# One ring of three PSUM banks for all background products, and both heads of a maximum unit as two 64-row products

## The reference

```
keys = einsum("bse,neh->bsnh", residual, W_key) + Bias_key          # queries, values alike
scores = einsum("bknh,bqnh->bnqk", keys, queries) / sqrt(H)
scores = where(q_idx < k_idx, 1e-10, scores)
probs = softmax(scores, axis=3)
weighted = einsum("bnqk,bknh->bqnh", probs, values)
out = einsum("bqnh,nhe->bqe", weighted, W_output) + Bias_output
x = x + attention(layernorm(x)); x = x + ffn(layernorm(x))          # ffn: 3 blocks of dequantised + low-rank linears
```

## Time and profile before

| | us |
|---|---|
| median of 3 runs | 2510.45 (2510.26 to 2524.81) |
| profiled execution, its own time | 2510.64 |
| its span | 2508.9 |
| attention, first score product to last weighted sum | 190.3 to 2117.6 |

### The profile page before, as it was taken

The page is one execution under the profiler, slowest core; times in us unless marked ns, Lnnn a source line. Parts: engine busy times, 40 slices in busy tenths (PEclk is TensorE's granted clock), DMA queues, the critical chain, the costliest instruction groups (busy, mean ns, idle before and its releaser), DMA issues. The chain is left out here.

```text
span 2508.9 us, 30066 instructions
## 1 busy us (share of the span) xinstructions
PE 2276.1 (91%) x9988; PEld 1172.2 (47%) x10080; DVE 1502.6 (60%) x3928; ACT 815.9 (33%) x1166; POOL 1183.0 (47%) x1075
## 2 busy tenths in 40 slices
PE   3479999999999999999999999999999997699987
PEld 2214444444444444444444444444444443577765
DVE  3584757575656565656565656666666665166664
ACT  1103333343333343433333333343333343001111
POOL 0105565656565657474747474747474720111110
PEclk8669999999999999999999999999999999799998
DMA  4463353626263536353544444444545341612100
GB/s 135 145 143 94 89 147 82 152 75 154 73 154 86 141 93 168 99 128 102 124 107 120 113 114 121 107 125 106 128 99 135 89 120 39 218 44 100 59 18 17
DMA packets 205354, 273.58 MB, mean 109 GB/s; under 512 B 69200, under 2 KB 86800, under 8 KB 205200
## 3 DMA queue, kind: packets, MB, share of 16 engines
q1 hardware_dynamic: 205200, 271.67, 41.4%
HBM read 176.69 MB, written 94.63 MB: 108 GB/s over the span
## 5 line engine op out<-in xcount | busy, mean ns | idle before, releaser
L691 POOL TENSOR_TENSOR acc<-acc,probs 128x512 f32<-128x512 f32 (+1 forms) x900 | 998.7, 1144 | 411.9 <-ACT probs L918 411.9
L918 ACT ACTIVATE probs<-ps_s 128x1024 f32<-128x1024 f32 (+2 forms) x640 | 552.6, 897 | 384.7 <-PE ps_s L780 230.2
L778 PE MATMUL ps_s<-qq,kk 128*128 128x512 f32 (+3 forms) x1280 | 638.3, 499 | 30.7 <-ACT probs L918 30.7
L967 DVE TENSOR_REDUCE partial<-ps_bg 128x1 f32<-128x512 f32 x768 | 513.6, 687 | 197.8 <-PE ps_bg L723 128.7
L799 PE MATMUL ps_o<-probs,v 128*64 128x512 f32 (+3 forms) x2560 | 537.8, 541 | 2.4 <-issue 2.4
L780 PE MATMUL ps_s<-qm,kl 128*128 128x512 f32 (+3 forms) x1280 | 468.4, 366 | 0.0
L723 PE MATMUL ps_bg<-k_bf,q_pad 128*128 128x512 bf16 (+3 forms) x1188 | 404.3, 362 | 57.3 <-DVE partial L967 18.8
L710 PE MATMUL ps_bg<-xs,w_in 128*128 128x512 f32 x768 | 366.9, 602 | 21.2 <-DMA xs<-xn_turned 18.8
L778 PEld LDWEIGHTS ps_s<-qq,kk 128*128 128x128 f32 x1280 | 247.4, 193 | 192.2 <-issue 118.5
L964 DVE CUSTOM_DVE_ANT_0 junk<-ps_bg,mask_q 128x512 bf16<-128x512 f32 (+3 forms) x512 | 242.4, 486 | 100.2 <-issue 94.1
L684 POOL TENSOR_TENSOR acc<-probs 128x512 f32<-128x512 f32 x90 | 112.8, 1275 | 401.1 <-ACT probs L918 401.1
(11 more groups left out here) (103 smaller groups left out, 1681.1 us busy)
## 6 DMA issues: line engine op xcount, KB each, us to landing
high_and_low<-split SPq DMA_DIRECT2D x128, 512.0 KB, 5.4
qq<-high_and_low SPq DMA_DIRECT2D x64, 512.0 KB, 4.7
kk<-high_and_low SPq DMA_DIRECT2D x128, 256.0 KB, 5.6
qm<-high_and_low SPq DMA_DIRECT2D x64, 256.0 KB, 6.3
kl<-high_and_low SPq DMA_DIRECT2D x64, 256.0 KB, 6.8
e<-masked_weights SPq DMA_DIRECT2D x128, 128.0 KB, 2.9
scale<-inverse_sums SPq DMA_DIRECT2D x128, 128.0 KB, 2.9
heads_turned<-o_out SPq DMA_DIRECT2D x64, 256.0 KB, 2.2
```

The lines of the kernel that those rows point to most:

```text
L691: g.tensor_tensor(acc[h][:, group % 2, q0:q0 + w], acc[h][:, group % 2, q0:q0 + w], probs[h][:, probs_slot(i, t), at:at + w], ALU.add).the ...
L778: pe.matmul(out, kk[:, h, kb * P:(kb + 1) * P], qq[:, h, q], start=True, stop=False, skip_group_check=True)
L918: nc.scalar.activation(probs[h][:, probs_slot(i, t), 0:width], ps_s[:, h, 0:width], ACT.Exp, scale=SCORE_SCALE).then_inc(p_ready, 1)
L967: e.reduce_max(to, ps_bg[:, n % 2, 0:w], AX.X).then_inc(max_read, 1)
```

## The change

It does three things.
- `ps_bg` gets three banks and `ps_fin` goes: projections, units, transposes and denominators take the three banks in turn, in the order in which TensorE issues them. A function `background` writes that order down, and every use waits for the reader of the use three before it.
- `q_pad` becomes one `q_bf` of both heads, as `k_bf` is. A unit is now both heads: two products over 64 rows each (`HEAD`), rows 0 to 63 and 64 to 127, into two banks in succession. There are 40 units for 80.
- The units start at slot 11 and end at slot 115. They take the keys of the last chunk first, so that each needs only the projections done by then.

```diff
-MAX_UNITS = [(h, qb, u, min(CH, 128 * (qb + 1) - CH * u))
-             for c in GROUPS for qb in range(4 * c + 3, 4 * c - 1, -1) for u in range(c + 1) for h in range(2)]
+MAX_UNITS = [(qb, u, min(CH, 128 * (qb + 1) - CH * u))
+             for c in GROUPS for u in range(c, -1, -1) for qb in range(4 * c + 3, 4 * c - 1, -1)]
...
-MAX_AT = [n + (n % 6 == 4) for n in range(MAX_SLOT, MAX_SLOT + NMAX)]
+MAX_AT = [11, 13, 15, 17, 19, 21, 25, 27, 29, 31, 33, 35, 38, 41, 44, 47, 50, 53, 56, 59, 61, 65, 68, 71, 75, 77, 80, 85,
+          87, 89, 92, 95, 97, 99, 101, 104, 109, 111, 113, 115]
...
+def background(n_pairs_in_all):
+    order = [("proj", 0, u) for u in range(NPROJ)] + [("max", 0, n) for n in range(NMAX)]
+    order += [(kind, 0, c) for kind, c in FIN_FIRST]
+    for i in range(n_pairs_in_all):
+        for n in range(SLOTS + 1):
+            if i + 1 < n_pairs_in_all:
+                order += [("proj", i + 1, u) for u in range(NPROJ) if PROJ_SLOT[u] == n]
+                order += [("max", i + 1, v) for v in range(NMAX) if MAX_AT[v] == n]
+            order += [(kind, pair_of(i, kind, c), c) for kind, c, at in FIN
+                      if at == n and pair_of(i, kind, c) < n_pairs_in_all]
+    first, users, counts = {}, [], {"proj": 0, "max": 0, "fin": 0}
+    for use in order:
+        kind = use[0] if use[0] in counts else "fin"
+        first[use] = len(users)
+        for _ in range(2 if kind == "max" else 1):
+            counts[kind] += 1
+            users.append((kind, counts[kind]))
+    return first, users
...
-        ps_bg = ctx.enter_context(nc.psum_tensor("ps_bg", [P, 2, CH], F32))
+        ps_bg = ctx.enter_context(nc.psum_tensor("ps_bg", [P, BANKS, CH], F32))
-        ps_fin = ctx.enter_context(nc.psum_tensor("ps_fin", [P, CH], F32))
+        place, users = background(N)
...
+                def bank_read(kind, j, n, h=0):
+                    k = place[kind, j, n] + h
+                    if k >= BANKS:
+                        reader, count = users[k - BANKS]
+                        pe.wait_ge({"proj": proj_read, "max": max_read, "fin": fin_read}[reader], START + count)
...
                 def max_unit(j, n):
-                    h, qb, u, w = MAX_UNITS[n]
...
-                    pe.matmul(ps_bg[:, n % 2, 0:w], q_pad[h][:, qb * P:(qb + 1) * P], k_bf[:, CH * u:CH * u + w],
-                              start=True, stop=True).then_inc(max_scores, 1)
+                    qb, u, w = MAX_UNITS[n]
+                    pe.wait_ge(bf_ready, START + 4 * j + PROJ_CHUNKS.index(u) + 1)
+                    for h in range(2):
+                        bank_read("max", j, n, h)
+                        pe.matmul(bank("max", j, n, h)[:, 0:w], q_bf[HEAD[h], qb * P:(qb + 1) * P],
+                                  k_bf[HEAD[h], CH * u:CH * u + w], start=True, stop=True).then_inc(max_scores, 1)
...
-                        for h in range(2):
-                            own = slice(64 * h, 64 * h + 64)
-                            e.tensor_copy(q_pad[h][own, cols(c)], part[own, 0, :].bitcast(F32))
+                        e.tensor_copy(q_bf[:, cols(c)], part[:, 0, :].bitcast(F32))
...
-                for h in range(2):
-                    e.memset(q_pad[h][:, :], 0.0)
```

More of the change, by code:

```diff
@@ L350, in attention @@
         vt = sb("vt", [P, S])
-        q_pad = [sb(f"q_pad{h}", [P, S], BF16) for h in range(2)]
+        q_bf = sb("q_bf", [P, S], BF16)
         k_bf = sb("k_bf", [P, S], BF16)
@@ L438, in fin_index, with bank @@
             return [e[:2] for e in FIN].index((kind, c))
+        def bank(kind, j, n, h=0):
+            return ps_bg[:, (place[kind, j, n] + h) % BANKS, :]
         def nth(i, group):
@@ L815, in between @@
                             continue
-                        before = fin_before(i, k)
                         if kind == "vt":
-                            turn_values(c, before)
+                            turn_values(values_pair(i, kind, c), c)
                         elif kind == "den":
-                            denominators(i, c, before)
+                            denominators(i, c)
                         else:
-                            turn_max(i + 1, c, before)
+                            turn_max(i + 1, c)
                 for u in range(NPROJ):
@@ L828, in _ @@
                     max_unit(0, n)
-                for k, (kind, c) in enumerate(FIN_FIRST):
+                for kind, c in FIN_FIRST:
                     if kind == "mt":
-                        turn_max(0, c, k)
+                        turn_max(0, c)
                     else:
-                        turn_values(c, k)
+                        turn_values(0, c)
                 for h in range(2):
@@ L944, in low @@
                     part = split[u // 3 % 2]
-                    e.scalar_tensor_tensor(part[:, 2 * m + 1, :], ps_bg[:, u % 2, :], bias[:, m:m + 1],
+                    e.scalar_tensor_tensor(part[:, 2 * m + 1, :], bank("proj", j, u), bias[:, m:m + 1],
                                            part[:, 2 * m, :].bitcast(F32), ALU.add, ALU.subtract
@@ L957, in take_max @@
                 def take_max(j, n):
-                    h, qb, u, w = MAX_UNITS[n]
-                    dve.wait_ge(max_scores, START + NMAX * j + n + 1)
-                    if u == qb // 4:
-                        e.memset(wait_here[:, n % 4:n % 4 + 1], 0.0)
-                    to = partial[:, h, qb, u:u + 1]
-                    if u == qb // 4:
-                        e.tensor_tensor_reduce(junk[:, n % 2, 0:w], ps_bg[:, n % 2, 0:w], mask_q[:, CH - w:CH], 1.0,
-                                               3 * NEVER, ALU.add, ALU.max, to).then_inc(max_read, 1)
-                    else:
-                        e.reduce_max(to, ps_bg[:, n % 2, 0:w], AX.X).then_inc(max_read, 1)
-                    c = qb // 4
+                    qb, u, w = MAX_UNITS[n]
+                    c = qb // 4
+                    for h in range(2):
+                        of = bank("max", j, n, h)[:, 0:w]
+                        k = (place["max", j, n] + h) % BANKS
+                        to = partial[:, h, qb, u:u + 1]
+                        dve.wait_ge(max_scores, START + 2 * (NMAX * j + n) + h + 1)
+                        if u == c:
+                            e.memset(wait_here[:, k:k + 1], 0.0)
+                            e.tensor_tensor_reduce(junk[:, k, 0:w], of, mask_q[:, CH - w:CH], 1.0,
+                                                   3 * NEVER, ALU.add, ALU.max, to).then_inc(max_read, 1)
+                        else:
+                            e.reduce_max(to, of, AX.X).then_inc(max_read, 1)
                     if n == LAST_MAX[c]:
-                        dve.wait_ge(max_read, START + NMAX * j + n + 1)
+                        dve.wait_ge(max_read, START + 2 * (NMAX * j + n + 1))
                         e.tensor_reduce(neg_max[:, c, :].rearrange("p (h r) -> p h r", h=2),
```

50 lines of the change are left out of this document (22 added, 28 removed).

## The result

| | median us | lowest to highest | n |
|---|---|---|---|
| before | 2512.02 | 2510.26 to 2524.81 | 6 |
| changed | 2444.61 | 2440.23 to 2557.76 | 6 |

The changed kernel is faster: ratio 0.9712, 95% interval 0.9681 to 0.9743. Predicted were 2448 us in a range of 2420 to 2530. In a second series the ratio is 0.9713 (0.9684 to 0.9742). All readings of "the changed kernel" here are from a profiled execution of the second series, span 2441.3 us.

What follows compares the result with a forecast made beforehand. TensorE's queue was taken as the bound. Per pair, 1.7 - 6.5 - 0.3 + 1.5 = -3.6 us, x 15 = -54, and -9 before the loop: -63 from 2510.6 gives 2448 us, range 2420 to 2530.

Steps and rivals of the forecast that it cites:

- Waits for banks: TensorE's waits at units for VectorE to read a bank, and for the last denominators' bank, go: -6.5 us a pair.
- stalls: Score products waiting 0.89 us behind slot 21's projection evacuation on ScalarE; the new unit there fills part: -0.3 us a pair.
- new waits: Three or four stalls of 0.3 to 0.5 us at slots 11 to 35, for a bank's earlier reader: +1.5 a pair.
- Halved products: Maximum products as 64-row halves overlap fully, but shape changes cost more: 15.0 us a pair for 13.3, +1.7.
- 0.10, 0.14 and 0.20: TensorE weight load per shape change: 0.10 us into bf16 products, 0.14 into the weighted sum, 0.20 into f32 products.
- Tiles: Sign in the attention loop: tiles 1 to 5 longer by about 0.9 us each (+4), tiles 6 to 17 shorter.
- Before the loop: Work ahead of the steady pairs: fewer clearings, faster first units and transposes, together -9 us.
- The clearings: Before the loop, two clearings of padded queries on VectorE, which first projections wait for, go: -1.9 us.
- serial halves: Rival: a unit's two row halves run one after the other, +109 us, 2557 us; chance 0.13.
- an emptied array: Rival: leaving a shape also empties TensorE's array, 0.17 us each, +135 us, 2583 us; chance 0.05.
- serial loads: Rival: a unit's two weight loads do not overlap, +4.0 us a pair, 2508 us; chance 0.09.
- its rival: Rival: the three banks stall projections, 3.6 us new waits, half the removed ones return, 2500 us; chance 0.13.

Runs made afterwards that it cites:

- the ring alone: The kernel before with only the three banks taken in turn, its 80 padded units in old order at old slots 35 to 114: ratio 0.9722.
- the halves undone: Changed kernel with three banks and new slots kept, but each unit again two padded 128-row products: usual executions 2441.8 and 2444.1 us, ratio 0.9703.
- units at the weighted sum: Changed kernel with 35 of its 40 units at slots 3 and 5 of a tile, directly before or behind the weighted sum: ratio 0.9786.
- the long execution: A profiled execution of the changed kernel itself, nothing altered, with the masked product of group 2 held up in 13 of 15 pairs: 2552.6 us.
- the last experiment: Changed kernel with masked product of group 2 at slot 49, inversion of group 3 at 91, its normalisation at 101, their transfers later: ratio 0.9979.
- late slots: Changed kernel with its 40 units at slots 35 to 113, three a tile, without the early start: 2471.7 to 2488.6 us, ratio 0.9860.

## Why the prediction was right

- **Waits for banks** (-6.5, stalls -0.3, new waits +1.5, together -5.3 a pair): blocks end late by 3.4 us for 8.8, -5.4. Right in sum. Of it, the stall behind slot 21 went from 0.97 to 0.64; new waits are 0.46 at a projection and 0.37 at a unit, nearer 1 than 1.5. The cause is shown by taking it away and by giving it alone: without the third bank a pair takes 9.6 us more, and the ring alone gives 3.7.
- **Halved products** (+1.7): the blocks' quickest lengths sum to 2.2 us more; measured against padded ones in the same slots TensorE is busy 1.4 to 2.0 more. Right as a price on TensorE's queue, and the surprising sign holds there: the halves overlap fully (6.3 us a pair, priced 7.3), and changes of shape eat more than that. As time it is not seen: with the halves undone the mean period stays at 119.5. Each price, 0.10, 0.14 and 0.20, was found again at the hundredth. The Trainium skill ("TensorEngine Tiling (Array Packing)", Key Properties) says that changing the tiling mode drains the engine. No cost beside the load is seen here: a unit ends 0.32 behind the score product, 0.10 + 0.216.
- These two sum to -3.2 of the -3.9 us a pair; 0.7 I could not place. The split is an estimate: with the blocks grouped in other ways the first is -4.3 to -6.5 and the second +0.5 to +2.6. Measured is the sum: -3.6 was predicted, period 119.8, and 119.47 came.
- **Tiles** (+0.9 in each of 1 to 5, the rest shorter): +1.6, +1.0, +0.5 and +1.5 in tiles 2 to 5, together 4.7 for 4, and 7.4 less in tiles 6 to 17.
- **Before the loop** (-9): -13.3, and the terms were mis-sized. The clearings (-1.9) gave nothing, since projections waited for `xs` and began 2.0 later; with the ring alone, which keeps the clearings, they began at 101.8, earlier than in either. From the first projection to the first unit it now takes 6.5 us less, a term I did not have: 3.6 of it are waits for VectorE that are gone (2.42 and 1.15), and the granted clock of this stretch is 0.92 for 0.86. The units gave 5.4 for 4 (49.4 to 44.0 from first to last start), the transposes 3.6 for 3 (8.5 to 4.9). That this part is off by 4 only is luck: the clearings and the later start are 3.9 the other way, and the 6.5 without a term cover them. Over the whole span 63 less was forecast and 67.6 came, from -4 here, -3 in the loop and +2.7 behind it.
- **Rivals**: serial halves, measured, take 2535 for 2557; an emptied array and serial loads are excluded by the 0.32 us of a unit and the 0.43 of the score product behind it. New stalls of the ring, 0.46 and 0.37, are far from the 3.6 us a pair of its rival.
- **Not foreseen**: VectorE being kept out by GpSimd. Five of the twelve executions took 2553 to 2581, above the range's upper end of 2530; no term of the sum stands for them. I wrote that GpSimd's busy time leaves slack. It does, but the steps of tiles 9 to 13 took 27.9 us and take 24.3, and hold 20 additions of 22.4 us: before, these stood as 8, 8 and 4 with gaps, now as one train.

## What to carry over

When an engine waits for a buffer's reader, a third buffer can be worth all of a change: try it alone first. Here the array trick beside it gave nothing that is seen in the time, and without the third buffer it cost more than it gave. A price on an engine's queue is not yet time: with padded products TensorE was busy less and then waited more. In this kernel a narrow product took its stream plus one weight load for every change of shape, in and out. After speeding up one engine, look at which other engine's work has become gapless, and which instructions must find a gap in it.

## What was not expected of the hardware

- A VectorE instruction with its tensors in SBUF that begins in a running GpSimd addition usually waits for that addition: it ends 0.55 us after the addition's end (1.34, 1.52, 1.00 us for 0.75, begun 0.49, 0.29 and 0.84 us into it). Begun 1.22 us into it, shortly before its end, it stayed out for the next one as well (1.86 us, units at the weighted sum). Begun 0.63 us into it, it took either 1.21 or 8.00 us, the latter until the train's end, in executions of one program and in pairs of one execution. The Trainium skill ("SBUF — State Buffer", Who interferes with whom) says that a VectorE instruction with two inputs in SBUF contends with a GpSimd instruction that reads SBUF, and calls their shared ports an exclusive lock; of VectorE's 2-port modes it says that whoever issues first has the ports for the whole instruction and the other fully blocks. The trace agrees for one addition; that the loser can stay out for six more is beyond it. All that were caught had begun 0.58 to 0.64 us into an addition. Why there, and what decides between 1.21 and 8.00, stays open. That this wait makes up all five long executions of the changed kernel is argued from the trace of one of them, not shown. With the halves undone two of four executions were long too, while in its profiled, usual one the masked product of group 2 began 0.26 us into an addition; no long one of that kernel was profiled.
- Short waits of TensorE in a busy stretch can be followed by 3.4 us or more at granted clock 0.5, on top of the wait. The 5.0 us of the long execution were followed by it in all 13 pairs (6.8 to 10.2 us of it, from before the wait's end on), the 3.2 us of the last experiment as well, waits of 2.0 us with units at the weighted sum in two of three cases, waits of 1.14 to 1.17 us with late slots in six of 15 pairs. Such a dip of 3.4 us makes a pair with late slots 1.6 us longer. In a quiet pair the clock is 1.00 throughout, also behind the wait of 1.16 us in tile 19.
